# Delta-rule stage: the last third of a block's work issued inside the next block, the gate computed in place, and centring two steps ahead in the layer norms

## The reference

```python
q, k, v = (_conv_silu(x @ W, conv) for W, conv in ((Wq, conv_q), (Wk, conv_k), (Wv, conv_v)))
g = -exp(A_log) * softplus(x @ Wfa @ Wfb + dt_bias)
beta = sigmoid(x @ Wb); qf = l2norm(q) * DH ** -0.5; kf = l2norm(k)
def step(state, inp):                     # along the tokens
    state = state * exp(g_i)
    inner = k_i . state
    state = state + (b_i * k_i) x (v_i - inner)
    return state, q_i . state             # o_i
o = o * rsqrt(mean(o * o) + EPS) * norm_w * sigmoid(x @ Wga @ Wgb)
out = o @ Wo                              # summed over the heads
```

## Time and profile before

| what | value |
|---|---|
| median of 3 runs | 8669.24 us (8667.85 to 8671.25) |
| the profiled execution | 8674.82 us, its span 8673.0 us |
| granted PE clock, mean over the span | 0.848 |
| busy share of the span | PE 78%, DVE 39%, ACT 33%, POOL 31% |
| the 32 blocks of kda | from 3457 to 6670 us of the span |

### The profile page before, as it was taken

How to read it: one execution, slowest core, us unless ns; L and a number is a source line. 1 busy time by engine, 2 the same in 40 slices (tenths; PEclk the granted TensorE clock), 3 DMA queues, 4 the chain that set the end, 5 groups by cost and what they waited for, 6 DMA issues and landing times. The chain is left out here.

```text
span 8673.0 us, 118859 instructions
## 1 busy us (share of the span) xinstructions
PE 6753.6 (78%) x49328; PEld 4649.2 (54%) x49328; DVE 3362.8 (39%) x4762; ACT 2897.8 (33%) x5331; POOL 2700.0 (31%) x1889
## 2 busy tenths in 40 slices
PE   6778776888547886777776777766777999989999
PEld 5566665666335663554544554544454444777444
DVE  3333334333334332444444444444444212545221
ACT  1211121333433333444443443443444112555211
POOL 3344333000000001555555555555554222000222
PEclk7777777888778887888888888888888999989999
DMA  0000000000000000000000000000001111000211
GB/s 20 0 0 0 0 0 24 0 0 0 11 24 0 0 0 13 12 12 12 12 12 17 12 12 12 12 12 16 13 12 57 43 43 30 0 0 0 84 39 47
DMA packets 57522, 132.00 MB, mean 15 GB/s; under 512 B 11126, under 2 KB 21366, under 8 KB 55898
## 3 DMA queue, kind: packets, MB, share of 16 engines
q1 hardware_dynamic: 57178, 126.63, 4.5%
HBM read 124.10 MB, written 2.50 MB: 15 GB/s over the span
## 5 line engine op out<-in xcount | busy, mean ns | idle before, releaser
L568 PE MATMUL ps<-moe_xn_all,moe_w 128*128 128x512 f32 x1792 | 808.2, 594 | 1.7 <-DVE moe_h L681 1.7
L1799 POOL TENSOR_TENSOR kda_rows<-kda_a,kda_f 128x512 f32<-128x512 f32 x225 | 365.1, 1623 | 1260.3 <-DVE kda_a L1780 1101.5
L568 PEld LDWEIGHTS ps<-moe_xn_all,moe_w 128*128 128x128 f32 x1792 | 340.2, 191 | 424.4 <-issue 421.6
L681 DVE TENSOR_TENSOR moe_h<-moe_silu,ps 128x512 f32<-128x512 f32 x224 | 153.9, 687 | 935.7 <-ACT moe_silu L623 928.6
L1751 DVE SCALAR_TENSOR_TENSOR kda_cv<-kda_pre,kda_w_front,kda_cv 128x1024 f32<-128x1024 f32 x297 | 508.1, 1727 | 19.0 <-ACT kda_cv L1693 15.4
L623 ACT ACTIVATE moe_silu<-ps 128x512 f32<-128x512 f32 x224 | 133.7, 597 | 986.0 <-PE ps L568 985.9
L524 POOL TENSOR_TENSOR moe_h<-moe_h,moe_cb 128x512 f32<-128x512 f32 x176 | 233.5, 1327 | 696.5 <-DVE moe_h L681 696.5
L578 PE MATMUL ps<-moe_h,moe_w 128*128 128x512 f32 x896 | 420.3, 592 | 0.0
L1626 PE MATMUL ps<-kda_fa_all,kda_w_front 128*128 128x512 f32 x132 | 129.3, 1111 | 365.4 <-issue 203.6
L1645 PE MATMUL ps<-kda_xn_all,kda_w_front 128*128 128x512 f32 x792 | 368.0, 608 | 48.7 <-ACT kda_gate L1685 44.4
L1799 POOL TENSOR_TENSOR kda_rows<-kda_q,kda_f 128x512 f32<-128x512 f32 x225 | 375.8, 1670 | 0.0
(11 more groups left out here) (483 smaller groups left out, 15799.2 us busy)
## 6 DMA issues: line engine op xcount, KB each, us to landing
kda_w_front<-in_Kw SPq DMA_DIRECT2D x33, 519.0 KB, 4.9
kda_col<-kda_beta SPq DMA_DIRECT2D x33, 512.0 KB, 4.1
moe_w<-in_Mw SPq DMA_DIRECT2D x6, 2816.0 KB, 19.4
moe_cb<-kda_beta SPq DMA_DIRECT2D x64, 256.0 KB, 3.2
moe_cb<-kda_beta SPq DMA_DIRECT2D x32, 224.0 KB, 3.0
moe_cb<-kda_beta SPq DMA_DIRECT2D x32, 192.0 KB, 2.8
moe_cb<-kda_beta SPq DMA_DIRECT2D x32, 160.0 KB, 2.7
moe_w<-in_Mw SPq DMA_DIRECT2D x6, 768.0 KB, 5.7
```

The costliest lines, as they stand in the source:

```text
L568: last = nc.tensor.matmul(ps_gu[u % 2][r], w13[:, k, i, r], n.xn[:, k, cols(c)], start=k == 0, stop=k == KD - 1)
L1799: nc.gpsimd.tensor_tensor(out, halves(src[:], h, 1), halves(o.f[:], h, 1), ALU.mult).then_inc(done, 1)
```

## The change

- The tail of a block (`tail_pe`, `tail_act`, `tail_dve`) is issued in the next block, between its levels, from `uf`, `aq`, `bg` and `v`, which now outlive the block; an extra block behind the loop does the last tail, and the first block does one on zeros. `d0` and `d1` are called `inner`, z `state`, e `right_side`. They share one PSUM bank (`ps_tail`, bank 5), one after the other, so each matmul group waits for the copy of the one before.
- The gate's matmul and sigmoid belong to the tail and come first in a block; the sigmoid writes `gated`, which is multiplied by y half by half.
- The PE's order in a block: gate, diagonal, scores(0), project(0), X of level 0, inner(0), decay, scores(1), state, then the levels with one tail piece in each. `scores(l + 1)` stands behind the level's `t_times_x` and projection, where it stood ahead. X of a level goes through one bank and one copy of 128x512 in place of two of 128x256.
- ACT's and DVE's orders are written out anew. The functions of the decay (log, exp) come early. `w_out` is loaded in each block, in two buffers, with the gate's weights.
- POOL's `first_level` is split: the two row products stay at a block's end (`first_rows`), the two that widen g and f open the next block.
- In the layer norm DVE centres step c + 2 ahead of step c's correction.

```diff
     centre(0)
+    centre(1)
     for c in range(LN_STEPS):
-        if c + 1 < LN_STEPS:
-            centre(c + 1)
+        if c + 2 < LN_STEPS:
+            centre(c + 2)
...
             def project(i):
                 if i == 0:
-                    pe.wait_ge(m.gate_in_sb, 1)
-                else:
-                    pe.wait_ge(m.proj_read, 2 * i)
+                    pe.wait_ge(free, count)
+                elif i == 1:
+                    pe.wait_ge(m.dec_in_sb, 1)
+                elif i == 2:
+                    pe.wait_ge(m.proj_read, 4)
...
+            def decay():
+                pe.wait_ge(m.proj_read, 2)
+                low_rank(w[:, K_FB:K_FB + P], fa_all, quad, m.dec_ready)
...
-        ps_bg, ps_z, ps_d1, ps_d0, ps_e, ps_y = bank4(0), bank4(0), bank4(1), bank4(2), bank4(3), two(4)
+        ps_tail = bank4(5)
...
+            def state():
+                pe.wait_ge(n.d_in_sb, 1)
+                for u in range(UNITS):
+                    last = nc.tensor.matmul(ps_tail[:, u], bg[:, u], d[:, 0, u], start=True, stop=True)
+                last.then_inc(n.z_ready, 1)
...
+            def square_sums(after, count):
+                pe.wait_ge(after, count)
+                pe.wait_ge(n.ysq, 2)
...
             for l in range(1, B_LEVELS):
-                lt_times_t(l, 0)
-                lt_times_t(l, 1)
-                if l < B_LEVELS - 1:
-                    scores(l + 1)
-                else:
-                    last_scores()
+                lt_times_t(l)
+                if l == 1:
+                    tail.y_of(0)
+                elif l == 2:
+                    tail.right_side()
+                elif l == 3:
+                    tail.inner(1)
                 t_times_x(l, 0)
                 t_times_x(l, 1)
                 if l < 3:
                     f.project(l)
+                elif l == 3:
+                    tail.y_of(1)
                 elif l == 4:
                     f.squares(0)
-            last_x(0)
-            last_x(1)
-            last_dt(0)
-            last_dt(1)
...
+                if l < B_LEVELS - 1:
+                    scores(l + 1)
+                else:
+                    last_scores()
+            last_x()
+            f.squares(1)
+            last_dt()
+            f.values()
...
+            tail.square_sums(m.vt_in_sb, 1)
             pe.wait_ge(n.uf_ready, 3)
...
+            tail.out()
```

More of the change, by code:

```diff
@@ L1617, in w_vec, with low_rank, front_pe @@
             return w[:, at:at + 1]
-        def front_pe(pe, o, w, quad):
+        def low_rank(w, rows, quad, done):
+            for hf in range(2):
+                last = nc.tensor.matmul(psum(g, FRONT + hf, BANK), w, rows[:, bass.ds(quad * QUAD + hf * BANK, BANK)],
+                                        start=True, stop=True)
+            last.then_inc(done, 1)
+        def front_pe(pe, o, w, quad, free, count):
             def half(i):
                 return bass.ds(quad * QUAD + i * BANK, BANK)
[L1624 to L1635, removed]
             def project(i):
                 if i == 0:
-                    pe.wait_ge(m.gate_in_sb, 1)
-                else:
-                    pe.wait_ge(m.proj_read, 2 * i)
+                    pe.wait_ge(free, count)
[3 more added lines that the diff above has]
+                    pe.wait_ge(m.proj_read, 4)
                 for hf in range(2):
@@ new lines, in last_dt @@
+            def last_dt():
+                pe.wait_ge(n.x_in_sb, B_LEVELS)
+                for at in range(MATS):
+                    last = nc.tensor.matmul(ps_dt6[lower, at], x_sb[upper, at], t[upper, at, 1], start=True, stop=True)
+                last.then_inc(n.dt_ready, 1)
+            tail.gate()
+            for at in range(MATS):
+                for b in range(2):
+                    own = slice((2 * (at // UNITS) + b) * HALF, (2 * (at // UNITS) + b + 1) * HALF)
+                    last = nc.tensor.matmul(ps_dg[corners[b], at], o.col[:, at % UNITS, own], o.q[:, at % UNITS, own],
+                                            start=True, stop=True)
@@ L2004, in chain_act @@
+            copy_x(1)
+            tail.square(0)
+            f.project(1)
+            f.log_decay()
+            copy_x(2)
+            f.inverse()
+            f.silu(0)
+            f.project(2)
+            copy_x(3)
+            f.square(0)
+            tail.square(1)
+            copy_x(4)
+            f.silu(1)
+            f.square(1)
+            copy_x(5)
             for c in range(QT):
@@ L2007, in chain_act @@
             f.silu(2)
-            f.square(1)
-            f.one_plus()
-            copy_x(B_LEVELS, 0, upper)
-            copy_x(B_LEVELS, 1, upper)
-            act.wait_ge(n.t_ready, 2 * B_LEVELS)
+            f.log_sum(0)
+            copy_x(B_LEVELS, upper)
+            f.log_sum(1)
+            act.wait_ge(n.e1_in_sb, 1)
+            f.values()
+            act.wait_ge(n.t_ready, 2 * B_LEVELS + 1)
             for b in corners:
                 nc.scalar.activation(uf[b, :, b], t[b, :, 1], ACT.Copy).then_inc(n.uf_ready, 1)
-            for c in range(QT):
-                act.wait_ge(n.dt_ready, 2 * (B_LEVELS - 1) + c + 1)
-                nc.scalar.activation(uf[lower, mats(c), upper], ps_dt[c][lower, :, 0], ACT.Copy).then_inc(n.uf_ready, 1)
+            act.wait_ge(n.dt_ready, 2 * (B_LEVELS - 1) + 1)
+            nc.scalar.activation(uf[lower, :, upper], ps_dt6[lower], ACT.Copy).then_inc(n.uf_ready, 1)
+            tail.log()
+            f.decays()
+            f.root(0)
+            f.root(1)
+            tail.root()
             act.wait_ge(n.sc_done, B_LEVELS)
@@ L2126, in chain_dve @@
+            update(2)
+            tail.right_side()
+            f.tap(1, 0)
+            masks(3)
+            f.tap(1, 1)
+            update(3)
+            tail.inner(1)
+            f.corr(0)
+            masks(4)
+            f.tap(1, 2)
+            update(4)
+            tail.gate(1)
+            f.corr(1)
+            f.tap(2, 0)
+            masks(5)
+            f.tap(2, 1)
+            update(5)
+            f.tap(2, 2)
+            last_masks()
             f.corr(2)
             f.q_row()
-            def residual(k):
-                dve.wait_ge(n.out_ready, k + 1)
-                xs = g.x_all[:, k, quad * QUAD:(quad + 1) * QUAD]
-                nc.vector.tensor_tensor(xs, two(2 * k), xs, ALU.add).then_inc(n.x_done, 1)
@@ L2216, in _ @@
                 f.clip()
-                for i, j in product(range(3), range(CONV - 1)):
+                for j in range(CONV - 1):
+                    f.tap(0, j)
+                for i in range(2):
+                    f.corr(i)
+                for i, j in product((1, 2), range(CONV - 1)):
                     f.tap(i, j)
-                for i in range(3):
-                    f.corr(i)
+                f.corr(2)
                 f.q_row()
```

541 lines of the change are left out of this document (272 added, 269 removed).

## The result

| kernel | median us | ratio to before, 95% interval | mean block of kda, us |
|---|---|---|---|
| before | 8670.24 (8667.85 to 8675.89) | | 100.6 |
| changed | 8757.13 (8747.58 to 8761.75) | 1.0098 [1.008, 1.0115] | 103.2 |

The forecast was 8747 us. The profiled execution took 8757 us over a span of 8755.5, with a mean granted clock of 0.844. The last column is the mean distance from one block's first PE group to the next one's, over blocks 2 to 31; half of these blocks stand behind the loop's jump and half don't.

The account below looks back on a forecast made before the run. No engine is full, so a chain of waits bounds the stage. Loop +77, last tail +38, clearing buffers +2 and norms -39 make +78 on the profiled 8674.8, 8753; the median, 5.6 lower, is 8747 us, range 8690 to 8810.

Parts of the forecast that it names:

- C: Block's end, from the last X: ACT's queue, then outputs and last residual; 28.8 us against 35.6, -6.8.
- A: Block's start to level 1's X: X starts at 18.3 us after a 2.3 us PE pause; +3.4.
- B: Levels 1 to 5: 45.0 us at full clock, 47.4 with one half-clock stretch; +3.6.
- loop: The 32 kda blocks: +2.4 us a block, +77 in all.
- last tail: Behind the loop: the tail runs alone at half clock, +38 us (30 to 44).
- norms: Layer norms: earlier centring saves 5 us in each of six plain ones, 9 in double ones; -39 us.
- memsets: Outside the blocks: clearing four more buffers, +2 us.
- fall in A: Block's start: PE's clock falls in two blocks of three, +2.2 us a block.
- one near level 5: Levels: one half-clock stretch near level 5, as before, adds 2.4 us a block.
- Rival 1: Blocks: PE keeps its clock, pauses being under 2.93 us; -3.4 a block, 8561 us; chance 0.27.
- That stays: Blocks behind the loop's jump: PE's late start and 2.22 us pause in the first group remain, left out of the difference.
- Rival 3: Blocks: DVE and POOL collide more, clock falls twice; +6.8 a block, 8888 us; chance 0.14.

Follow-up runs that it names:

- ln_only: The kernel before with only the layer norm's centring issued two steps ahead: 8637.0 us, ratio 0.9959 to before.
- mask1: The changed kernel with DVE's first convolution tap moved behind the masks of level 1: 8692.05 us, ratio 1.0027 to before.
- early: The changed kernel with the next level's scores ahead of `t_times_x` and its masks ahead of the updates: 8558.86 us, ratio 0.9867 to before.
- fillA: The changed kernel with 14 unread matmuls on PE in its wait for level 1's mask: 8672.2 us, ratio 1.0002 to before.
- fillC: The changed kernel with 40 unread matmuls on PE in its wait for the scaling, ahead of the output matmuls: 8630.24 us, ratio 0.9955 to before.
- combo2: The changed kernel with earlier scores, masks, tail root and scaling, later first tap, reordered ACT copies and logarithm, and 18 unread matmuls before the outputs: 8104.95 us.
- no_last_tail: The changed kernel without the extra block behind the loop, so the last tail is left out: 8730.9 us, ratio 1.0066 to before.

## Why the prediction was right, step by step

Means of the 15 blocks of each kind, from the PE groups' starts; C runs to the next block's first group.

| | A | B | C with barrier | block |
|---|---|---|---|---|
| before, not behind the jump | 14.85 | 43.80 | 42.06 | 100.7 |
| changed, same | 18.87 | 49.06 | 37.28 | 105.2 |
| before, behind the jump | 18.40 | 44.29 | 37.79 | 100.5 |
| changed, same | 18.99 | 49.00 | 33.16 | 101.2 |

**The sum.** +2.4 a block was forecast and +2.6 to 2.7 measured; loop +77 and +87, last tail +38 and +36.8, norms -39 and -34.5 (ln_only) to -37 (like marks of the traces), memsets and first front +2 and some -4 (the first front's sigmoid and low-rank group are gone, which I hadn't counted). The sum is 10 us short, nearly all of it the loop's. By parts, over all blocks, A was forecast at +3.4 and came to +2.3, B with the clock +5.8 and +5.0, C -6.8 and -4.7. So the direction, the last tail and the norms are right by their terms, but that the loop's mean is so near is partly luck: misses of both signs met in it.

The forecast's 96.4 us from start to start runs from PE's first group to POOL's first row of the next block. PE's own next start is later, 99.9 us in that block. It did no harm: the blocks ahead of the jump have 4.3 us more in C than the others before, and 4.1 after.

**Part A.** 18.3 forecast, 18.9 measured, but of the 15 blocks not behind the jump none is near that mean. In nine of them the first group takes 3.75, as forecast, and A is 19.9: the diagonal group behind it is at half clock too (1.98 for the 1.1 forecast), and the pause is 3.0 to 3.2 for 2.3. In the other six the first group takes 1.95, and A is 17.3:

```profile
3739.90 1.96 PE L1625 MATMUL ps<-kda_ga_all,kda_w_out 128*128 128x512 f32 x4 [3.01 <-PEq L76]
3741.79 1.15 PE L2012 MATMUL ps<-kda_q,kda_col 128*64 128x64 f32 x32
```

Behind the jump the pause is 2.42. mask1 shows the tap as its cause. What stood behind it was missed: take the tap away and ACT's exponential is next.

**Part B.** The levels at full clock were forecast at 9.3, 10.5, 9.1, 9.6, 6.5; the trace has 9.5, 10.75, 9.3, 9.1, 6.7 in its fastest blocks, a sum of 45.3 for 45.0. early shows that the late scores and mask are their reason.

**The clock.** A fall in A in two of three blocks and one near level 5 were forecast at 4.6 us a block. Level 1 is over 10.8 us in 27 of 30 blocks, and levels 1 and 5 together are 3.8 us above their full-clock length. So the fall in A came more often than forecast and cost less each time. fillA shows that in level 1 the pause brings it about: filled, X comes at 1.15 in all blocks. Rival 1 is refuted: its claim, that pauses under the 2.93 of the earlier trace rows leave the clock alone, fails at 2.42, with X at 1.97 us in 13 of the 15 blocks behind the jump. In the other two, and in 11 of 15 in fillC, the same pause was followed by X at full clock:

```profile
5309.77 1.15 PE L1982 MATMUL ps<-kda_t,kda_lt 64*64 64x64 f32 x32 [2.42 <-DVE kda_lt L2126]
```

So the pause's length doesn't decide by itself; what else does was not tested.

**Part C.** The step that failed by size: 28.8 to the last residual, measured 31.4, and -6.8 turned into -4.7. The scaling begins at 21.8, as forecast, but takes 2.39 and not 1.1, and the outputs take 5.9 and not 5.2. I had priced DVE's rows at 1.2 to 1.7 for POOL's presence and then the scaling, the one beside POOL's first row, as if alone. And the forecast's own terms, 21.9, 1.1, 5.2 and 1.4, add up to 29.6 and not 28.8: 0.8 of the 2.6 is a slip in the sum. Added up rightly they give +3.2 a block and 8773 us, too high by more than the forecast was too low.

**The loop's jump.** "That stays" was wrong. Blocks behind the jump had 3.55 us more in part A; in the changed kernel it is 0.1, with no pause of 2.22 in the first group. So the blocks not behind the jump became 4.5 us longer and those behind it 0.7, and this gain of 1.7 a block, with B's 0.8, made up for part C's 2.1. That is the luck in the loop's mean. Why the pause is gone is shown by no run here; it stays open.

**Table loads.** Seven a block, each 1.28 us; the one at 4649.78 begins 0.02 behind the logarithm and ends where the decays start, at 4651.07. The drain of 1380 ns of the Trainium skill (ScalarE: Activation LUTs, "What ACT_TABLE_LOAD costs") is in no row here, before or after.

**Rival 3** had both falls of the clock but priced them on top of the forecast; the collision with POOL was real, in the scaling.

## What to carry to other kernels

When work is moved into gaps, write down for each engine what now stands ahead of the instruction that others wait for: here nearly the same instructions in another order (and two more table loads a block) are 7.5% faster than the changed kernel (8104 beside 8757 us). A pause that one engine causes often hides the next engine's; removing it shows its successor, so forecast the second in line too. And price a faster clock, or filler that keeps it, only where PE's work ends the stretch.

## What the runs showed of the hardware

A pause of PE of 2.42 us was followed by X at 1.97 us instead of 1.15 in 13 of 15 blocks, and with 3.29 us of unread matmuls in its place by 1.15 in all. The clock's fall is thus a cost of its own beside the pause: 1.6 us a block in level 1 and 2.1 in level 5 here.

DVE's multiplication with both inputs in SBUF took 2.39 us beside POOL's row of 2.46, and 1.22 with POOL idle; two residuals, with one input in PSUM, took 2.36 together beside POOL's rows in combo2. The Trainium skill (SBUF — State Buffer, "Who interferes with whom") says that a DVE instruction with two SBUF inputs contends with a POOL instruction that reads SBUF, and the other waits until the first is done; these rows agree.

The same loop body comes in different lengths within one execution: blocks not behind the jump are near 103 us where their first group takes 1.95 and near 106 or more where it takes 3.75. How many are of each kind differs between executions: six of 15 in the changed kernel's trace and one in no_last_tail's, whose loop is the same, a difference of 0.8 us a block. A difference of that size between two profiled executions therefore shows nothing by itself.
